# Self attention of a decoder block: queries and keys projected transposed, rotated pairs swapped and split parts stacked by SBUF-to-SBUF DMAs

## The chip, the cores and the metric

The kernel runs on one core of a Trainium2 chip. The time is the device time of one execution in microseconds (us): 1643.54 us before the change, the median of three runs (1643.11 to 1645.99). Engines are named as in the profile: PE is TensorE (matmuls; PEld its weight loads), DVE is VectorE, ACT is ScalarE, POOL is GpSimd, SP is SyncE, which here only issues DMAs.

## What is computed

A decoder block on x of 4 batches x 512 tokens x 512: self attention, cross attention over 1601 context rows, and a mixture of experts, each followed by residual and layer norm. The change touches self attention alone:

```python
q, k, v = (proj(Wq), proj(Wk), proj(Wv))          # 16 heads of 32
q = q * cos + _rotate_half(q) * sin               # _rotate_half: (x0, x1) -> (-x1, x0), pair by pair
k = k * cos + _rotate_half(k) * sin
att = softmax(q @ k.T / sqrt(32) + causal mask)
out = (att @ v).reshape(B, T, D) @ Wo.T
```

## The kernel before

Every matmul operand is split into a high part in fp32r and the rest in fp32r (`x_sp`, `wqkv`, `wo`, index 0 and 1), and a product is three matmuls (`PASSES`: hi*hi, hi*lo, lo*hi). For scores the three products are made in one matmul: for a head (32 features) the parts hi, hi, lo of q stand on 96 partitions above each other in `q_st`, and hi, lo, hi of k in `k_st`, so that one contraction over 96 rows sums all three.

The work goes in 16 groups, 4 heads of one batch each (`g = b * HG + hg`). For a group TensorE makes, in this order:

- 32 transposes (L496) of the split and rotated q and k (`qk_sp`, tokens on partitions) into `proj_ps`; ACT and DVE copy them to `q_st` (L253) and `k_st` (L362)
- `scores` (L446, the mask added by L448): 16 score tiles, n = qt * 4 + h, of 128 queries by 128 to 512 keys, in two PSUM buffers of `score_ps`; for each DVE takes the row maximum (L371, `maxed`), and the tile n waits for the maximum of n - 2
- the negated maxima are transposed (L520, `max_turned`) and copied as rows 96 to 127 of `q_st` (L260 on ACT, L391 on DVE), so that the second product comes out with the maximum subtracted
- `scores_t` (L462, mask L464): the scores again, keys on partitions; ACT takes the exponential (L268, `exped`) into `p_t`; behind it `values` (L471) and `weight_sums` (L478)

The projection of the next group (48 matmuls of 384 columns, L415: q, k and v of 4 heads for a token tile, tokens on partitions) is laid between these steps by hand, 5 matmuls behind each pair of scores, 7 and 6 around the first `scores_t`. When it is done ACT copies v (L232), DVE rotates (`rotate`, L305 to L312; the swap of pairs is a reversed access pattern on PSUM) and the parts are split by ACT, DVE and POOL (L201). Once a batch the output projection `project_out` (48 matmuls of 512 columns, L428) stands behind the scores of the next batch's first group.

SP loads x of a batch as one DMA, the weights in chunks through three places in `p_t`, and `rows` (4 MB, x by rows, for the residual), which is issued at 17.5 us. DVE waits for `rows_in` before its first group; PE starts when all weights are split (`w_lo`, 5 loads).

## Time and profile before

| | |
|---|---|
| median of 3 runs | 1643.54 us |
| the profiled execution: its span, first to last instruction | 1642.0 us |
| PE busy | 1421.5 us (87% of the span) |
| DVE, ACT, POOL busy | 993.8, 659.1, 271.0 us |
| mean granted TensorE clock | 0.937 of full speed |
| self attention: first matmul, last `weight_sums` | 26.4 us, 563 us |

A row of the timeline gives start, length, engine, line and operation, the tiles, the shape, the count of merged instructions, and in brackets how long the engine had been idle and what ended it. Matmuls overlap in their pipeline, so the time from one start to the next, not the length, is what one costs. PEclk is the granted clock of TensorE, 1.00 the upper of its two levels (2.4 GHz), 0.50 the lower (1.2 GHz). Self attention is a third of the span; what follows it (cross attention from 584 us, experts) begins when it has ended and is not changed.

### The profile page before, as it was taken

Reading aid. Unit: us, or ns where it says so; the run is one execution under the profiler, and the core shown is the slowest. Engines: PE = TensorE matmul, PEld = TensorE weight load, DVE = VectorE, ACT = ScalarE, POOL = GpSimd, SP = SyncE. Lnnn points to the kernel's source line nnn. Section 1 sums busy time; section 2 is a strip of 40 time slices with the busy share of each in tenths; the row PEclk is TensorE's granted clock in tenths of the full one; section 3 lists DMA queues with packets and bytes.
Section 4 is the critical chain, followed back from the end, with each engine's and each line's share of the span. In section 5 each row is a group of like instructions: output and inputs, shape, how many; then the busy total and the mean of one; then the engine's idle time right before and its main releaser. Section 6 shows DMA issues by size and latency. Waiting matters only on the chain. (4 is left out here: it accounts for less than half of the span.)

```text
span 1642.0 us, 25753 instructions
## 1 busy us (share of the span) xinstructions
PE 1421.5 (87%) x9093; PEld 1174.7 (72%) x9093; DVE 993.8 (61%) x1677; ACT 659.1 (40%) x1042; POOL 271.0 (17%) x233
## 2 busy tenths in 40 slices
PE   2898998998999758999898985499999999998890
PEld 2665676666766447788787874389999999997770
DVE  4665565565665483444434427777777777775677
ACT  3344233244334223333323314266566655664222
POOL 1002001001000020200102000122222222221762
PEclk9999999999999779999999998589999999999995
DMA  6000000000000032220312004177877878784654
GB/s 268 1 1 26 1 2 27 2 1 1 1 1 1 1 138 83 74 87 16 104 40 77 23 1 142 46 265 276 287 277 275 299 271 292 275 273 178 196 165 142
DMA packets 61589, 190.29 MB, mean 116 GB/s; under 512 B 7112, under 2 KB 7116, under 8 KB 60624
## 3 DMA queue, kind: packets, MB, share of 16 engines
q1 hardware_dynamic: 48880, 147.93, 24.6%
q0 software_dynamic: 12640, 41.43, 8.4%
q8 instruction: 45, 0.74, 0.2%
q14 instruction: 24, 0.20, 0.0%
HBM read 156.30 MB, written 33.03 MB: 115 GB/s over the span
## 5 line engine op out<-in xcount | busy, mean ns | idle before, releaser
L415 PE MATMUL proj_ps<-wqkv,x_sp 128*128 128x384 f32 x768 | 174.5, 362 | 26.4 <-DVE wo L297 26.4
L1510 DVE TENSOR_TENSOR e_w_sp<-e_w_raw,e_w_sp 128x1024 fp32r<-128x1024 f32 x141 | 168.7, 1221 | 18.1 <-ACT e_w_sp L1468 11.3
L952 PE MATMUL c_score_ps<-ct,x_t 128*128 128x402 f32 x768 | 155.4, 364 | 0.0
L952 PEld LDWEIGHTS c_score_ps<-ct,x_t 128*128 128x128 f32 x768 | 149.8, 201 | 6.9 <-issue 6.1
L1454 POOL DMA_INDIRECT e_x_g<-x_rows,e_index x94 | 101.2, 1076 | 323.7 <-DVE e_index L1521 309.1
L415 PEld LDWEIGHTS proj_ps<-wqkv,x_sp 128*128 128x128 f32 x768 | 135.2, 200 | 26.4 <-issue 26.4
L1468 ACT ACTIVATE e_w_sp<-e_w_raw 128x1024 fp32r<-128x1024 f32 x141 | 145.9, 1058 | 16.8 <-DMA e_w_raw<-w_experts 16.6
L992 PE MATMUL c_out_ps<-cr,weigh_t 128*128 128x512 f32 (+1 forms) x624 | 152.5, 399 | 0.0
L1569 PEld LDWEIGHTS e_gate_ps<-e_x_t,e_w_sp 128*128 128x128 f32 x1128 | 140.6, 191 | 5.9 <-DVE e_x_t L1531 1.8
L1569 PE MATMUL e_gate_ps<-e_x_t,e_w_sp 128*128 128x256 f32 x1128 | 142.1, 283 | 1.4 <-DVE e_x_t L1531 1.4
L1569 PE MATMUL e_up_ps<-e_x_t,e_w_sp 128*128 128x256 f32 x1128 | 143.3, 283 | 0.0
L371 DVE TENSOR_REDUCE row_max<-score_ps 128x1 f32<-128x128 f32 (+3 forms) x256 | 114.3, 483 | 47.8 <-PE score_ps L448 46.2
L1595 PE MATMUL e_down_ps<-e_w_sp,e_h_sp 128*128 128x512 f32 x564 | 139.0, 396 | 0.0
L1569 PEld LDWEIGHTS e_up_ps<-e_x_t,e_w_sp 128*128 128x128 f32 x1128 | 135.1, 188 | 0.0
L992 PEld LDWEIGHTS c_out_ps<-cr,weigh_t 128*128 128x128 f32 (+1 forms) x624 | 115.2, 188 | 25.7
L268 ACT ACTIVATE p_t<-score_ps 128x512 f32<-128x512 f32 (+3 forms) x256 | 102.2, 437 | 61.4 <-PE score_ps L464 59.6
L1595 PEld LDWEIGHTS e_down_ps<-e_w_sp,e_h_sp 128*128 128x128 f32 x564 | 102.6, 188 | 21.4
L877 DVE TENSOR_TENSOR weigh_t<-c_turn_ps,weigh_t 128x512 fp32r<-128x512 f32 x64 | 34.7, 584 | 134.1 <-ACT weigh_t L780 134.1
L780 ACT ACTIVATE weigh_t<-c_turn_ps 128x512 fp32r<-128x512 f32 x64 | 29.4, 513 | 196.5 <-PE c_turn_ps L973 196.5
L446 PE MATMUL score_ps<-k_st,q_st 96*128 96x256 f32 (+2 forms) x256 | 87.6, 399 | 16.8 <-POOL x_sp L195 8.6
L462 PE MATMUL score_ps<-q_st,k_st 128*128 128x256 f32 (+2 forms) x256 | 92.5, 413 | 8.5 <-ACT p_t L268 7.7
L462 PEld LDWEIGHTS score_ps<-q_st,k_st 128*128 128x128 f32 x256 | 50.2, 196 | 67.0 <-ACT p_t L268 62.4
(211 smaller groups left out, 2242.6 us busy)
## 6 DMA issues: line engine op xcount, KB each, us to landing
e_w_raw<-w_experts SPq DMA_DIRECT2D x141, 512.0 KB, 5.6
y_rows<-e_y SPq DMA_DIRECT2D x47, 512.0 KB, 2.9
raw<-ctxT SPq DMA_DIRECT2D x16, 800.5 KB, 4.3
raw<-ctx_rows SPq DMA_DIRECT2D x16, 768.0 KB, 4.8
x_raw<-xT SPq DMA_DIRECT2D x4, 1024.0 KB, 4.8
rows<-x_rows SPq DMA_DIRECT2D x1, 4096.0 KB, 14.2
x_rows<-rows SPq DMA_DIRECT2D x4, 1024.0 KB, 6.2
out<-rows SPq DMA_DIRECT2D x4, 1024.0 KB, 5.3
```

The source lines that it names most:

```text
L268: nc.scalar.activation(p_t[:, h, p_at[kc]:p_at[kc] + w], score_ps[:, n % 2, kc * P:T], ACT.Exp, scale=float(HD) ** -0.5).then_inc(exped, 1)
L371: nc.vector.tensor_reduce(row_max[:, qt, h:h + 1], score_ps[:, n % 2, 0:(qt + 1) * P], AX, ALU.max).then_inc(maxed, 1)
L415: mm = nc.tensor.matmul(proj_ps[:, tt, 0:GW], x_sp[:, xs, c, tt * P:(tt + 1) * P], wqkv[:, ws, c, hg * GW:(hg + 1) * GW], start=(c == 0 an ...
L446: nc.tensor.matmul(score_ps[:, n % 2, 0:wide], q_st[0:3 * HD, h, qt * P:w], k_st[0:3 * HD, h, 0:wide], start=True, stop=False)
L462: nc.tensor.matmul(score_ps[:, n % 2, q0:T], k_st[:, h, kc * P:(kc + 1) * P], q_st[:, h, q0:T], start=True, stop=False)
L952: mm = nc.tensor.matmul(score_ps[:, f, 0:MQ], x1_t[:, xs, c, qt * P:(qt + 1) * P], ct[:, cs, c, f * MQ:(f + 1) * MQ], start=False, stop=(c ...
L992: mm = nc.tensor.matmul(out_ps[:, qt % 2, :], weigh_t[0:k, ws, c, :], cr[0:k, cs, c, :], start=(c == 0 and m == 0), stop=(c == MC - 1 and ...
L1454: nc.gpsimd.indirect_dma_start(x_g[:, par, half, :], None, x2_rows, bass.IndirectOffsetOnAxis(ap=index[:, par, half:half + 1], axis=0)).th ...
L1468: nc.scalar.activation(w_sp[:, par, part, 0, :], w_raw[:, par, part, :], ACT.Copy).then_inc(w_hi[part], 1)
L1510: nc.vector.tensor_tensor(w_sp[:, par, part, 1, :], w_raw[:, par, part, :], w_sp[:, par, part, 0, :].bitcast(F32), ALU.subtract).then_inc( ...
L1569: mm = nc.tensor.matmul(ps[:, par, i, :], w_sp[:, par, part, ws, at:at + P], x_t[:, par, xs, c, :], start=(c == 0 and n == 0), stop=(c == ...
L1595: mm = nc.tensor.matmul(down_ps[:, half, :], h_sp[:, par, hs, i, half * P:(half + 1) * P], w_sp[:, par, DOWN, ws, i * D:(i + 1) * D], star ...
```

## The change

Queries and keys of 4 heads are projected with features on partitions and the 512 tokens along the row: weights are the stationary operand, 12 matmuls of 512 columns for q and 12 for k (L464 of the new kernel), into `qk_ps`. The values of a whole batch are projected apart, 48 matmuls of 512 columns (`project_v`; `values_ahead` behind the scores of the last group of the batch before; at the start in one pass with q and k). TensorE's transposes and the copies out of them are gone.

What was a reversed access pattern is now data movement over partitions: ACT copies the projection to `qk_raw`, SP issues two DMAs for each of q and k that swap even and odd partitions into `qk_swapped` (`swap`, 64 partitions x 2 KB each), POOL multiplies `qk_raw` by cos, DVE multiplies `qk_swapped` by sin and adds, ACT takes the high part, POOL the low part (into the place of `qk_swapped`). Then `put_together` fills `q_st` and `k_st`: for each head three DMAs for q and three for k, 24 DMAs of 32 partitions x 2 KB (64 KB) a group. As `q_st` and `k_st` exist once, SP waits before them for the last `scores_t` of the group before (`scored_t`, g * SC). Scores of heads 0 and 1 wait for the first 12 DMAs (`stacked[0]`), those of heads 2 and 3 for the second 12 (`stacked[1]`), and the next group's swap for all 24.

The output projection and the values use `job_ps`, two PSUM banks of their own. x comes in four DMAs a batch (into the free half of `v`), `woT` through `v` as well; `woT` and `rows` are issued behind `put_together(0)`. The loops over batches are written out.

```diff
+        def stack_places(h):
+
+            part = slice(h * HD, (h + 1) * HD)
+            for s, splits in ((Q, (hi, hi, lo)), (K, (hi, lo, hi))):
+                for n, src in enumerate(splits):
+                    yield stack[s][n * HD:(n + 1) * HD, h, :].bitcast(F32), src[part, s, :].bitcast(F32)
+
+        STACKED = 2 * 2 * 3 * 16
...
-                sp.dma_start(rows[:, :, :], x).then_inc(rows_in, 16)
-                with sp.Fori(1, B) as b:
-                    sp.wait_ge(x_lo, b)
-                    sp.dma_start(x_raw[:, :, :], xT[b]).then_inc(x_in, 16)
...
+                def swap(g, s):
+                    sp.wait_ge(copied, g * 2 + s + 1)
+                    if g >= 1:
+                        for pair in range(GH // 2):
+                            sp.wait_ge(stacked[pair], g * STACKED)
+                    for odd in range(2):
+                        sp.dma_start(swapped[odd:P:2, s, :], raw[1 - odd:P:2, s, :]).then_inc(swap_in[s], 16)
+
+                def put_together(g):
+                    sp.wait_ge(hi_done, g * 2 + 2)
+                    sp.wait_ge(lo_done, g * 2 + 2)
+                    if g >= 1:
+                        sp.wait_ge(scored_t, g * SC)
+                    for h in range(GH):
+                        for dst, src in stack_places(h):
+                            sp.dma_start(dst, src).then_inc(stacked[h // 2], 16)
+
...
+                swap(0, Q)
+                swap(0, K)
+                put_together(0)
+                sp.wait_ge(x_lo, DC)
+                sp.dma_start(v[:, 1, :, :].rearrange("p t d -> p (t d)"), woT).then_inc(wo_in[0], 16)
+                sp.dma_start(rows[:, :, :], x).then_inc(rows_in[0], 16)
+                for g in range(NG - 1):
+                    b, hg = g // HG, g % HG
+                    swap(g + 1, Q)
+                    swap(g + 1, K)
+                    if hg == 1 and b + 1 < B:
...
+                    put_together(g + 1)
...
+                def times_cos(g, s):
+                    pool.wait_ge(swap_in[s], (g + 1) * 32)
+                    if g == 0:
+                        pool.wait_ge(tables_in, 32)
+                    nc.gpsimd.tensor_tensor(raw[:, s, :], raw[:, s, :], cos_t[:, :], ALU.mult).then_inc(by_cos, 1)
+
+                def lo_qk(g, s):
+                    pool.wait_ge(hi_done, g * 2 + s + 1)
+                    nc.gpsimd.tensor_tensor(lo[:, s, :], raw[:, s, :], hi[:, s, :].bitcast(F32), ALU.subtract
+                                            ).then_inc(lo_done, 1)
...
+                def copy_raw(g, s):
+                    act.wait_ge(projected, g * 2 + s + 1)
+                    if g >= 1:
+                        act.wait_ge(lo_done, (g - 1) * 2 + s + 1)
+                    nc.scalar.activation(raw[:, s, :], qk_ps[:, s, :], ACT.Copy).then_inc(copied, 1)
+
+                def hi_qk(g, s):
+                    act.wait_ge(rotated, g * 4 + 2 * s + 2)
+                    if g >= 1:
+                        for pair in range(GH // 2):
+                            act.wait_ge(stacked[pair], g * STACKED)
+                    nc.scalar.activation(hi[:, s, :], raw[:, s, :], ACT.Copy).then_inc(hi_done, 1)
...
-                            if n == 1 and not last:
-                                keep_v(g + 1, (hg + 1) % 2)
+                            if n == GH + 1 and not last:
+                                hi_qk(g + 1, Q)
                             if n == 2 * GH + 1 and not last:
-                                hi_q(g + 1)
...
-                        nc.vector.tensor_tensor(qk_cos[:, s, :, :], proj_ps[:, :, part], cos_t[:, :, :],
-                                                ALU.mult).then_inc(roped, 1)
-                        swapped = proj_ps[:, :, part].rearrange("p t (n two) -> p t n two", two=2)[:, :, :, ::-1]
-                        nc.vector.tensor_tensor(qk_sin[:, s, :, :].rearrange("p t (n two) -> p t n two", two=2),
-                                                swapped, sin_t[:, :, :].rearrange("p t (n two) -> p t n two", two=2),
-                                                ALU.mult).then_inc(roped, 1)
...
+                def rotate(g, s):
+                    dve.wait_ge(swap_in[s], (g + 1) * 32)
+                    if g == 0:
+                        dve.wait_ge(tables_in, 32)
+                    nc.vector.tensor_tensor(swapped[:, s, :], swapped[:, s, :], sin_t[:, :], ALU.mult
+                                            ).then_inc(rotated, 1)
+                    dve.wait_ge(rotated, g * 4 + 2 * s + 1)
+                    dve.wait_ge(by_cos, g * 2 + s + 1)
+                    nc.vector.tensor_tensor(raw[:, s, :], raw[:, s, :], swapped[:, s, :], ALU.add
+                                            ).then_inc(rotated, 1)
...
-                    dve.wait_ge(scored_t, g * GH * TT)
-                    for h in range(GH):
-                        dve.wait_ge(turned, g * 2 * GH + 2 * h + 2)
-                        nc.vector.tensor_copy(k_st[0:3 * HD, h, :], proj_ps[0:3 * HD, (2 * h + 1) % 4, :]
-                                              ).then_inc(k_stacked, 1)
...
+                for s in (Q, K):
+                    rotate(0, s)
+                dve.wait_ge(*rows_in)
+                for g in range(NG):
+                    b, hg = g // HG, g % HG
+                    last = g == NG - 1
+                    if g >= 1:
+                        for part in range(3):
+                            invert_sums(g - 1, part)
+                        finish_out(g - 1)
...
-                            if n % 2 == 1 and n < 2 * GH and not first:
-                                if n // 2 < 3:
-                                    invert_sums(g - 1, n // 2)
-                                elif n // 2 == 3:
-                                    finish_out(g - 1)
...
-                products = [(tt, c, n) for tt in range(TT) for c in range(DC) for n in range(3)]
-
-                def project(g, hg, start, stop):
-
-                    for tt, c, n in products[start:stop]:
-                        xs, ws = PASSES[n]
-                        mm = nc.tensor.matmul(proj_ps[:, tt, 0:GW], x_sp[:, xs, c, tt * P:(tt + 1) * P],
-                                              wqkv[:, ws, c, hg * GW:(hg + 1) * GW],
+                products = [(c, n) for c in range(DC) for n in range(3)]
+                jobs = [0]
+
+                def project(g, s, start, stop):
+
+                    at = s * D + g % HG * P
+                    for c, n in products[start:stop]:
+                        ws, xs = PASSES[n]
+                        mm = nc.tensor.matmul(qk_ps[:, s, :], wqkv[:, ws, c, at:at + P], x_sp[:, xs, c, :],
                                               start=(c == 0 and n == 0), stop=(c == DC - 1 and n == 2))
-                        if c == DC - 1 and n == 2:
-                            mm.then_inc(projected, 1)
+                    if stop == len(products):
+                        mm.then_inc(projected, 1)
...
+                def project_v(b, tt, into, chunks=range(DC)):
+
...
+                                                  wqkv[:, ws, c, 2 * D:3 * D], start=(c == 0 and n == 0),
...
+                def values_ahead(b):
+
+                    if b == 1:
+                        pe.wait_ge(v_copied, TT)
+                    else:
+                        pe.wait_ge(res_added, (b - 1) * TT)
+                    pe.wait_ge(x_lo, split_x(b, DC - 1))
+                    for tt in range(TT):
+                        if tt >= 2:
+                            pe.wait_ge(v_copied, b * TT + tt - 1)
+                        project_v(b, tt, job_ps)
...
+                    if qt == 0:
+                        pe.wait_ge(stacked[h // 2], (g + 1) * STACKED)
+                    if n >= 2:
+                        pe.wait_ge(maxed, g * SC + n - 1)
+                    elif g >= 1:
+                        pe.wait_ge(exped, g * SC)
+                    else:
+                        pe.wait_ge(v_copied, TT)
...
-                    for n in range(2 * GH):
-                        h, s = n // 2, n % 2
-                        if n == 1:
-                            pe.wait_ge(k_lo, g + 1)
-                        if n >= 4:
...
-                        for tt in range(TT):
-                            mm = nc.tensor.transpose(proj_ps[0:3 * HD, n % 4, tt * P:(tt + 1) * P].bitcast(F32R),
-                                                     qk_sp[:, s, tt, h, :, :].rearrange("p n d -> p (n d)"),
-                                                     ident_r[:, :])
-                        mm.then_inc(turned, 1)
...
+                for c in range(DC):
+                    pe.wait_ge(w_lo, c + 1)
+                    pe.wait_ge(x_lo, c + 1)
+                    for s in (Q, K):
+                        project(0, s, c * 3, c * 3 + 3)
+                    for tt in range(TT):
+                        project_v(0, tt, (job_ps, score_ps)[tt // 2], [c])
+                pe.wait_ge(const_ready, 3)
+                for g in range(NG):
+                    b, hg = g // HG, g % HG
+                    last = g == NG - 1
+                    if not last:
+                        pe.wait_ge(copied, g * 2 + 1)
+                        if hg == HG - 1:
+                            pe.wait_ge(x_lo, split_x(b + 1, DC - 1))
+                        project(g + 1, Q, 0, len(products))
+                        pe.wait_ge(copied, g * 2 + 2)
+                    for n in range(SC):
+                        scores(g, n // GH, n % GH)
+                        if not last and n < len(products):
+                            project(g + 1, K, n, n + 1)
+                    if hg == 0 and b >= 1:
+                        project_out(b - 1)
                     if hg == HG - 1 and not last:
-                        pe.wait_ge(x_lo, b + 2)
-                    STEP = 5
-                    for n in range(2 * TT):
-                        scores(g, n // 2, n % 2)
-                        if n == 1 and not last:
-                            pe.wait_ge(q_stacked, g * GH + GH)
-                            pe.wait_ge(k_stacked, g * GH + GH)
-                        if n >= 1 and not last:
-                            project(g + 1, (hg + 1) % HG, (n - 1) * STEP, n * STEP)
-                    if hg == 0 and not first:
-                        project_out(b - 1)
-                    at = (2 * TT - 1) * STEP
-
-                    pe.wait_ge(max_lo, g + 1)
-                    if hg == 0 and not first:
-                        pe.wait_ge(res_added, b * TT)
-                    pe.wait_ge(o_scaled, g)
+                        values_ahead(b + 1)
+
+                    pe.wait_ge(negated, g * 2 + 2)
+                    if g >= 1:
+                        pe.wait_ge(o_scaled, g)
                     for qt in range(TT):
                         mm = nc.tensor.transpose(den_ps[:, qt * P:(qt + 1) * P].bitcast(F32R),
                                                  neg_max[:, qt, :, :].rearrange("p h n -> p (h n)"), ident_r[:, :])
                     mm.then_inc(max_turned, 1)
-                    if not last:
-                        project(g + 1, (hg + 1) % HG, at, at + 7)
-                    pe.wait_ge(maxed, g * GH * TT + GH * TT)
-                    scores_t(g, 0, 0)
-                    if not last:
-                        project(g + 1, (hg + 1) % HG, at + 7, len(products))
-                    scores_t(g, 0, 1)
+                    pe.wait_ge(maxed, g * SC + SC)
+                    for half in range(2):
+                        scores_t(g, 0, half)
+                    if g == 0:
+                        pe.wait_ge(v_copied, TT)
                     for kc in range(1, TT):
                         scores_t(g, kc, 0)
-                        values(g, hg, kc - 1)
+                        values(g, kc - 1)
                         scores_t(g, kc, 1)
                         weight_sums(g, kc - 1)
-                    values(g, hg, TT - 1)
+                    values(g, TT - 1)
                     weight_sums(g, TT - 1).then_inc(summed, 1)
-
-                pe.wait_ge(const_ready, 3)
-                pe.wait_ge(w_lo, W_LOADS)
-                pe.wait_ge(x_lo, 1)
-                project(0, 0, 0, len(products))
-                groups(group, lambda: project_out(B - 1))(pe)
+                project_out(B - 1)
```

SyncE, from the third weight chunk to the `rows` load, before:

```order
L167 DMA p_t<-wqkvT 128x1536 x3
L169 DMA cos_t<-rope 128x512
L170 DMA sin_t<-rope 128x512
L167 DMA p_t<-wqkvT 128x1536
L167 DMA p_t<-woT 128x2048
L171 DMA rows<-x_rows 128x8192
```

and the same place now: after the last weight chunk the swaps of group 0 (four DMAs in one row), the stacking of its four heads (the six rows from L175 `x2` on are one head), and only then `woT` and `rows`:

```order
L181 DMA p_t<-wqkvT 128x1536
L166 DMA qk_swapped<-qk_raw 64x512 x4
L175 DMA q_st<-qk_hi 32x512 x2
L175 DMA q_st<-qk_swapped 32x512
L175 DMA k_st<-qk_hi 32x512
L175 DMA k_st<-qk_swapped 32x512
...
L189 DMA v<-woT 128x2048
L190 DMA rows<-x_rows 128x8192
L166 DMA qk_swapped<-qk_raw 64x512 x4
```

28 DMAs have come ahead of `woT` and `rows`, and 28 more follow for every further group.

TensorE, from the last 512-wide score tile of a group (L446 before, L518 now) to the first tiles of the second product (L462, L534), before:

```order
L446 MATMUL score_ps<-k_st,q_st 128x512
L448 MATMUL score_ps<-mask_qk,ident_b 128x128
L415 MATMUL proj_ps<-wqkv,x_sp 128x384 x5
L520 MATMUL den_ps<-ident_r,neg_max 128x128 x4
L415 MATMUL proj_ps<-wqkv,x_sp 128x384 x7
L462 MATMUL score_ps<-q_st,k_st 128x512
```

and now:

```order
L518 MATMUL score_ps<-k_st,q_st 128x512
L520 MATMUL score_ps<-mask_qk,ident_b 128x128
L587 MATMUL den_ps<-ident_r,neg_max 128x128 x4
L534 MATMUL score_ps<-q_st,k_st 128x512
L536 MATMUL score_ps<-mask_kq,ident_b 128x128
```

No projection stands between these steps any more: q's 12 matmuls stand ahead of the group's scores, k's one by one behind the first 12 score tiles.

## Rows read from the trace of the kernel before

**Rows 1.** The first line of the page
```profile
span 1642.0 us, 25753 instructions
```

**Rows 2.** Windows: two whole groups and a stretch of the last; columns in its first line
```profile
core 0: us, PE busy (x) PEld busy (x) DVE busy (x) ACT busy (x) POOL busy (x), PEclk, DMA share, GB/s
...
504.28:533.15 28.87, 27.27 (x216) 19.17 (x213) 18.46 (x36) 11.78 (x25) 2.56 (x2) 1.00 0.00 1
...
533.15:563.00 29.85, 25.33 (x168) 14.17 (x164) 13.39 (x29) 10.68 (x23) 1.27 (x1) 0.77 0.00 1
...
541.70:555.30 13.60, 11.34 (x36) 5.43 (x35) 5.77 (x11) 4.54 (x8) 1.21 (x1) 0.50 0.01 2
```

**Rows 3.** Timeline of TensorE, second group, last but one: start, length, what, count
```profile
73.24 2.67 PE L496 MATMUL proj_ps<-ident_r,qk_sp 128*96 128x128 f32 x32
...
503.11 0.23 PE L464 MATMUL score_ps<-mask_kq,ident_b 128*128 128x128 bf16 x1
...
504.28 2.68 PE L496 MATMUL proj_ps<-ident_r,qk_sp 128*96 128x128 f32 x32
...
519.41 1.45 PE L415 MATMUL proj_ps<-wqkv,x_sp 128*128 128x384 f32 x7
...
520.71 0.40 PE L462 MATMUL score_ps<-q_st,k_st 128*128 128x512 f32 x1
```

**Rows 4.** Timeline of TensorE, the last group
```profile
535.66 0.35 PE L446 MATMUL score_ps<-k_st,q_st 96*128 96x256 f32 x1
...
536.89 0.35 PE L446 MATMUL score_ps<-k_st,q_st 96*128 96x256 f32 x1 [0.56 <-DVE row_max L371]
...
547.22 0.75 PE L520 MATMUL den_ps<-ident_r,neg_max 128*128 128x128 f32 x4 [1.22 <-DVE neg_max L383]
...
562.41 0.40 PE L478 MATMUL den_ps<-p_t,ones 128*32 128x128 f32 x8
```

**Rows 5.** Timeline of the SP queue: issues that follow each other at once
```profile
2.95 0.44 SPq L169 DMA_DIRECT2D cos_t<-rope  x1
...
3.44 0.49 SPq L170 DMA_DIRECT2D sin_t<-rope  x1
...
582.92 1.29 SPq L697 DMA_DIRECT2D raw<-ctxT  x3
```

**Rows 6.** DMA issues by line: count, KB each, us from issue to landing
```profile
bias<-expert_bias SPq DMA_DIRECT2D x1, 8.0 KB, 1.8
...
rows<-x_rows SPq DMA_DIRECT2D x1, 4096.0 KB, 14.2
```

**Rows 7.** Timeline of TensorE at a batch boundary
```profile
269.11 0.58 PE L446 MATMUL score_ps<-k_st,q_st 96*128 96x256 f32 x1 [2.90 <-POOL x_sp L195]
```

**Rows 8.** Timeline of the start, several engines
```profile
5.69 1.91 ACT L226 ACTIVATE x_sp<-x_raw 128x2048 fp32r<-128x2048 f32 x1 [3.56 <-DMA x_raw<-xT]
...
7.76 1.48 ACT L282 ACTIVATE wqkv<-p_t 128x1536 fp32r<-128x1536 f32 x1 [0.17 <-DMA p_t<-wqkvT]
...
19.50 1.76 DVE L297 TENSOR_TENSOR wqkv<-p_t,wqkv 128x1536 fp32r<-128x1536 f32 x1 [2.35 <-ACT wqkv L282]
...
26.42 10.09 PE L415 MATMUL proj_ps<-wqkv,x_sp 128*128 128x384 f32 x48 [26.42 <-DVE wo L297]
...
47.65 0.47 DVE L371 TENSOR_REDUCE row_max<-score_ps 128x1 f32<-128x128 f32 x2
```

**Rows 9.** Groups by line and shape, self attention: busy us, mean ns; idle before
```profile
L232 ACT ACTIVATE v<-proj_ps 128x512 f32<-128x512 f32 x15 | 9.0, 597 | 5.1 <-PE proj_ps L415 5.1
...
L201 POOL TENSOR_TENSOR qk_sp<-qk_cos,qk_sp 128x512 fp32r<-128x512 f32 x15 | 19.2, 1282 | 273.7 <-ACT qk_sp L238 273.7
...
L305 DVE TENSOR_TENSOR qk_cos<-proj_ps,cos_t 128x512 f32<-128x512 f32 x30 | 20.6, 688 | 34.1 <-ACT v L232 17.9 <-PE proj_ps L415 16.2
```

**Rows 10.** Timeline of TensorE, output projection of the last batch
```profile
572.62 2.96 PE L428 MATMUL den_ps<-wo,o_sp 128*128 128x512 f32 x12
...
575.42 2.96 PE L428 MATMUL o_ps<-wo,o_sp 128*128 128x512 f32 x12
```

382 lines of the change are left out of this document (189 added, 193 removed).

## The prediction

> **What bounds the kernel now.** I read the windows over whole groups first, then TensorE's timeline inside one, then the SP queue and the landings. In a group in the middle of self attention TensorE is busy 27.27 of 28.87 us at the full granted clock [rows 2]: it is the bound, because projection matmuls of the next group fill its waits for DVE's maxima and ACT's exponentials. The last group has nothing to fill with: it takes 29.85 us though it makes 48 matmuls fewer, and for 13.60 us of it the granted clock is 0.50 [rows 2]. That group is my model for the new one. Self attention ends at 563 us of a span of 1642.0 us [rows 1, 2]; what follows starts when it has ended and keeps its length.
>
> **Removed from TensorE.** The 32 transposes of a group go: 2.5 us (504.28 to 506.8, one 2.68 us piece less its pipeline [rows 3]). A 384-column matmul costs (520.71 - 519.41) / 7 = 0.186 us [rows 3], a 512-column one (575.42 - 572.62) / 12 = 0.233 us [rows 10]. Before 48 x 0.186 = 8.9 us of projection a group; now 24 x 0.233 = 5.6 us a group and 48 x 0.233 = 11.2 us a batch for the values, together 8.4. As work this is 3.0 us a group less. ACT and DVE lose four copies each, which only TensorE's next step waited for.
>
> **Added: the stacking wait.** I call T the end of a group's `weight_sums`. The last `scores_t` of a group starts at 503.11 and is done 0.9 us before T = 504.28 [rows 3]; only then may SP begin the 24 stacking DMAs. It issues them in order, and an issue occupies SP: three in a row took 1.29 us, 0.43 each, two loads of 2 KB rows started 3.44 - 2.95 = 0.49 apart [rows 5]. Theirs have 128 partitions, these 32; I take 0.41. The low bound is the 0.23 us that 64 KB take at the rate of the 4096 KB load (14.2 us [rows 6]), the high one 0.49. From last issue to landing I take 2.0 us: 1.8 for 8 KB [rows 6] and 0.2 for the bytes. So the first 12 DMAs have landed at T - 0.9 + 11 x 0.41 + 2.0 = T + 5.6, all 24 at T + 10.5. TensorE has only q's projection in between, 12 x 0.233 = 2.8 us: it waits from T + 2.8 to T + 5.6, does two score tiles, and waits for the third until T + 10.5. Some 7 us a group have no cover. Everything else of the new chain does: q is copied and swapped while SP and DVE wait anyway, k's projection ends with the twelfth tile, and swap, cos (POOL 1.28), sin and sum (DVE 0.69 each), the splits (ACT 0.60, POOL 1.28) [rows 9] come to some 8 us against more than 12 us from there to the last `scores_t`. If that cover failed, ACT would stand at `hi_qk` with the exponentials queued behind it, and `scores_t` with them. The next swap is queued on SP behind all 24 DMAs, which delays nothing that is late.
>
> **Added: the lost filling.** From the third score tile to the end the last group takes 562.4 - 536.9 + 0.3 = 26 us [rows 4], half of it at clock 0.50. The new group has this stretch with ten of k's matmuls in it (2.3 us at the full clock, most inside waits for maxima), and DVE's inversion of the sums moved ahead of the tiles, where the stacking wait covers it (some 1 us less). I take 27 us. The clock: TensorE got 0.50 from 541.70 on after several short waits [rows 2], and at a batch boundary a wait of 2.90 us [rows 7] came before half-speed matmuls; every new group has two such waits, so half the stretch at 0.50 stays in my 27. Bounds: 24 (full clock nearly throughout) and 31 (half throughout).
> A new group is then 10.5 + 27 = 37.5 us against 28.87: +8.6.
>
> **Batches.** Three times 11.2 us of values come in as a block of their own behind the scores: +33.5. Their block covers the wait for the maxima, 1.2 us and the clock around it [rows 4]: -4.5. Before, the 14 groups from 73.24 to 533.15 [rows 2, 3] took 459.9 us, where 14 x 28.87 + 3 x 11.2 (output projection) are 437.8: 22 us went at batch boundaries, mostly in the wait for POOL's split of x [rows 7] and the half clock behind it. The new order splits x two groups ahead in four pieces: -21.
>
> **The start.** TensorE now begins when a first chunk is split: 1 MB lands by 5.69, then ACT's split of 1.48 and DVE's of 1.76 [rows 8], so at 9 instead of 26.4, with 72 x 0.233 + 1.1 us of slow start (48 x 0.186 took 10.09 before [rows 8]), q and k ready at 24. Copies 1.2, swap 2.8, the rotation and splits as above give 32.6; 24 issues end at 42.5. Only then `woT` and `rows` are issued, and DVE does not take a maximum before `rows` has landed, 14.2 us later [rows 6]: 57 against 47.65 before [rows 8]. With 0.6 for two maxima and 27 the second group begins at 84.7, before at 73.24: +11.5.
>
> **Sum.** Start +11.5; 14 groups x 8.6 = +120; batches +33.5 - 4.5 - 21 = +8; the last group 10.5 + 25.5 = 36 against 29.85: +6. Together +145.5, so the profiled execution's 1642.0 becomes 1788, and the median of the runs, 1.5 above it, 1789.
>
> The Trainium skill bears on the dearest term twice. "DMA: Bandwidth & Descriptors", section "Issuing engines are not separate DMA queues", holds the sequencer's time for starting a DMA to be usually small beside the transfer. By these rows it is not: 0.43 us of issue against 0.23 us of bytes. By that rule the stacking would run at the transfers' pace, the second rival below. "SBUF — State Buffer", section "The DMA setup-cost knee", says a loop of 64 KiB transfers moves about 30% of what one of 4 MiB does; from its 395 GB/s an estimate of 0.55 us a DMA, 24 landed at T + 13.8, and the sum would be 1789 + 3.3 x 15 = 1838. No run here shows 64 KB DMAs yet.
>
> **Rivals.**
> 1. The waits vanish (issues of about 0.1 us). Nothing in the rows speaks for it: the shortest mean issue is 0.43. Then a group is 2.8 + 0.3 + 26.5 = 29.6, +0.7 x 14 = 10, with start +8, batches +8 and the last group -2: 1642 + 24, so 1667. 0.07.
> 2. The transfers set the pace, not the issues: 23 x 0.23 = 5.3, all landed at T + 6.4, a group of 33.4. 15 x 4.1 = 61 less, 4 less at the start: 1724. For it: these DMAs have a quarter of the rows of those in the trace. Against: issues in the trace differ little between loads of 256 KB and 800 KB. 0.15.
> 3. Slower than forecast: rows of 2 KB among 32 partitions go below the rate of the big load, or the half clock holds through the group (31): 10.5 + 31 or 14.5 + 27 are +4 a group, 15 x 4 = 60: 1849. For it: the granted clock of the last group. 0.15.
> 4. The other side, faster: TensorE stays busy as now and takes only its work. Its place is the score phase: it decides if stacks land before T + 2.8, 24 DMAs in 2 us, and the removed 3.0 us a group are not lost again to maxima and exponentials. Then 16 x 3.0 = 48 and the 21 of the boundaries are saved, the start gains nothing: 1643.5 - 69 = 1574. Against it the last group before, which lost to these waits all that 48 matmuls had cost. 0.03.
> 5. The change does not do what it says: not likely here; the DMAs are in the program in the order that the text shows.
>
> **How the numbers follow.** My forecast has 0.60. Its own range is 1750 to 1835 (issue 0.35 to 0.47, stretch 26 to 29). The range for 8 in 10 goes from rival 2 to rival 3 with a margin for 24 and 31 together with them: 1705 to 1865. A measurement of this kernel tells 0.2% (3 us) from no change. Faster only by rival 4 and a corner of rival 1: 0.04; within 0.2%: 0.01; slower: 0.95.
>
> **What would show it.** In the changed trace: SP's stacking issues about 0.41 us apart, beginning within 0.2 us of a group's last `scores_t`; TensorE idle before the first score tile about 2.8 us and before the third about 4 us, released by DMA, in each of 15 groups; group periods near 37.5 us; the clock 0.50 in a large part of them, mean below 0.937; the first maximum of DVE near 57 us, released by `rows`; self attention ending near 709 us; everything behind it as long as before. I am wrong if the period is below 33 us (issues faster, or the clock holds), or if TensorE's longest waits name ACT or DVE instead of a DMA (the rotation chain is late after all).

## The result and the profile after

| | before | after |
|---|---|---|
| median of four runs | 1644.76 us (1643.11 to 1646.12) | 1875.01 us (1871.06 to 1876.39) |
| ratio, 95% interval | | 1.1397 [1.138, 1.1413] |
| span of the profiled execution, mean granted clock | 1642.0 us, 0.937 | 1874.6 us, 0.859 |
| end of self attention | 563 us | 796 us |

The forecast was 1789 us with 1705 to 1865 for 8 in 10. The sign was right, and the time lies 10 us above the range. All of the loss is in self attention (796 - 563 = 233 us, as much as the spans differ).

The first lines of the page after, against [rows 1]:

```profile
span 1874.6 us, 24131 instructions
PE 1477.0 (79%) x8389; PEld 1149.6 (61%) x8389; DVE 935.6 (50%) x1548; ACT 649.6 (35%) x1038; POOL 348.2 (19%) x294
```

TensorE's timeline at the joint of two groups in the middle, where [rows 3] are of before (L464 is q's projection, L518 a score tile):

```profile
370.42 0.41 PE L545 MATMUL o_ps<-p_t,v 128*32 128x128 f32 x8
370.64 0.40 PE L552 MATMUL den_ps<-p_t,ones 128*32 128x128 f32 x8
370.98 3.01 PE L464 MATMUL qk_ps<-x_sp,wqkv 128*128 128x512 f32 x12
379.19 0.55 PE L518 MATMUL score_ps<-k_st,q_st 96*128 96x256 f32 x1 [5.20 <-issue]
380.21 0.41 PE L518 MATMUL score_ps<-k_st,q_st 96*128 96x256 f32 x1
...
386.77 0.58 PE L518 MATMUL score_ps<-k_st,q_st 96*128 96x256 f32 x1 [5.47 <-DMA k_st<-qk_hi]
```

With T = 370.98, the first score tile starts at T + 8.2 and the third at T + 15.8. The forecast had T + 5.6 and T + 10.5. SP's queue over the same joint, 12 issues of the 24 shown:

```profile
370.12 1.19 SPq L175 DMA_DIRECT2D q_st<-qk_hi  x2
371.36 0.59 SPq L175 DMA_DIRECT2D q_st<-qk_swapped  x1
371.99 0.59 SPq L175 DMA_DIRECT2D k_st<-qk_hi  x1
372.62 0.59 SPq L175 DMA_DIRECT2D k_st<-qk_swapped  x1
373.26 0.59 SPq L175 DMA_DIRECT2D k_st<-qk_hi  x1
373.89 1.22 SPq L175 DMA_DIRECT2D q_st<-qk_hi  x2
375.15 0.60 SPq L175 DMA_DIRECT2D q_st<-qk_swapped  x1
...
384.66 0.59 SPq L175 DMA_DIRECT2D k_st<-qk_hi  x1
386.80 1.15 SPq L166 DMA_DIRECT2D qk_swapped<-qk_raw  x2
```

An issue occupies SP for 0.59 us, and the next starts 0.63 us after it began; this distance is called the pitch below. The 24 of them from 370.12 to 385.25 take 15.1 us, where 24 x 0.41 = 9.8 were forecast. The first starts 0.3 us after the last `scores_t` tile (369.81). The landings, from the page, answer to [rows 6]:

```profile
qk_swapped<-qk_raw SPq DMA_DIRECT2D x64, 128.0 KB, 2.1
q_st<-qk_hi SPq DMA_DIRECT2D x128, 64.0 KB, 2.0
k_st<-qk_hi SPq DMA_DIRECT2D x128, 64.0 KB, 2.0
```

TensorE's longest waits from 100 to 800 us (total, times, longest):

```profile
PE score_ps L518 <- DMA k_st<-qk_hi: 92.3, 16, 8.1
PE score_ps L518 <- issue: 75.3, 14, 6.5
PE den_ps L587 <- DVE neg_max L434: 13.2, 9, 2.3
```

"issue" at L518 is the wait before the first score tile: TensorE waits for `stacked[0]`, and the profile names no event for it. The two together are 168 us. One group, from its first score tile to the next group's, cut at the third, answers to [rows 2]:

```profile
379.19:386.77 7.58, 2.10 (x7) 1.20 (x7) 0.58 (x2) 0.00 (x0) 0.00 (x0) 0.50 0.39 97
386.77:422.10 35.33, 33.29 (x190) 21.54 (x191) 13.31 (x23) 11.59 (x25) 5.12 (x4) 0.92 0.05 18
```

At the start the first maximum waits for `rows`, which SP could issue only behind the stacks ([rows 8] for before):

```profile
50.94 0.46 SPq L190 DMA_DIRECT2D rows<-x_rows  x1
65.45 0.49 DVE L427 TENSOR_REDUCE row_max<-score_ps 128x1 f32<-128x128 f32 x2 [32.77 <-DMA rows<-x_rows]
```

### The profile page after: what moved, and what is told of

Its sections match the earlier page's. It is cut to its first block and busy times, and to the rows that moved or that the text cites. A ratio compares the mean times of both kernels' runs of the same rounds, so it can differ in the third digit from the quotient of the medians.

```text
span 1874.6 us, 24131 instructions
## 1 busy us (share of the span) xinstructions
PE 1477.0 (79%) x8389; PEld 1149.6 (61%) x8389; DVE 935.6 (50%) x1548; ACT 649.6 (35%) x1038; POOL 348.2 (19%) x294
## 5 line engine op out<-in xcount | busy, mean ns | idle before, releaser
L518 PE MATMUL score_ps<-k_st,q_st 96*128 96x256 f32 (+2 forms) x256 | 114.4, 450 | 205.3 <-DMA k_st<-qk_hi 92.3
L427 DVE TENSOR_REDUCE row_max<-score_ps 128x1 f32<-128x128 f32 (+3 forms) x256 | 122.4, 490 | 281.4 <-PE score_ps L520 243.3
L518 PEld LDWEIGHTS score_ps<-k_st,q_st 96*128 96x128 f32 x256 | 66.3, 259 | 230.9 <-issue 115.0
L464 PE MATMUL qk_ps<-x_sp,wqkv 128*128 128x512 f32 x384 | 170.5, 523 | 9.3 <-DVE wqkv L365 9.3
L282 ACT ACTIVATE qk_raw<-qk_ps 128x512 f32<-128x512 f32 x32 | 19.1, 597 | 348.3 <-PE qk_ps L464 348.2
L534 PE MATMUL score_ps<-q_st,k_st 128*128 128x256 f32 (+2 forms) x256 | 116.1, 504 | 20.8 <-ACT q_st L339 13.2
L534 PEld LDWEIGHTS score_ps<-q_st,k_st 128*128 128x128 f32 x256 | 59.3, 232 | 97.0 <-issue 48.5
L464 PEld LDWEIGHTS qk_ps<-x_sp,wqkv 128*128 128x128 f32 x384 | 91.2, 241 | 19.4 <-DVE wqkv L365 9.2
```

The lines of the kernel that those rows point to most:

```text
L427: nc.vector.tensor_reduce(row_max[:, qt, h:h + 1], score_ps[:, n % 2, 0:(qt + 1) * P], AX, ALU.max).then_inc(maxed, 1)
L464: mm = nc.tensor.matmul(qk_ps[:, s, :], wqkv[:, ws, c, at:at + P], x_sp[:, xs, c, :], start=(c == 0 and n == 0), stop=(c == DC - 1 and n = ...
L518: nc.tensor.matmul(score_ps[:, n % 2, 0:wide], q_st[0:3 * HD, h, qt * P:w], k_st[0:3 * HD, h, 0:wide], start=True, stop=False)
L534: nc.tensor.matmul(score_ps[:, n % 2, q0:T], k_st[:, h, kc * P:(kc + 1) * P], q_st[:, h, q0:T], start=True, stop=False)
```

## The experiments

All ratios are to the kernel before, run on the same chip, with a 95% interval. Times are medians of four to six runs, but single runs where this is said. A "plain" group has no block of 48 matmuls (values or output projection).

**Fewer, larger DMAs.** High and low parts lie in one tensor, q's and k's stacks in another, so that one DMA serves both.

```diff
-            for s, splits in ((Q, (hi, hi, lo)), (K, (hi, lo, hi))):
-                for n, src in enumerate(splits):
-                    yield stack[s][n * HD:(n + 1) * HD, h, :].bitcast(F32), src[part, s, :].bitcast(F32)
+            for n, src in enumerate((slice(0, 3, 2), slice(0, 4, 3), slice(1, 3, 1))):
+                yield stack[n * HD:(n + 1) * HD, :, h, :].bitcast(F32), parts[part, src, :]
```

> The four parts of q and k lie in one tensor and q_st and k_st in another, so that one DMA of 32 partitions x 2 x 2 KB takes the place of two: 12 stacking DMAs of 128 KB a group instead of 24 of 64 KB, same bytes. Theory A (an SBUF-to-SBUF issue costs SP 0.63 us whatever it moves): the stacks have landed 12 x 0.63 = 7.6 us earlier in each of 16 groups, 1875 - 16 x 7.6 = about 1753, issues still 0.63 apart. Theory B (the pace is that of bytes or packets, the queue pushes back): issues 1.26 apart and 1875 as now. The swaps, 128 KB each and 0.62 apart in the changed kernel's trace, speak for A.

1761.76 us, ratio 1.0708 [1.069, 1.0726]. Half the DMAs with twice the bytes: the pitch stays.

```profile
411.75 8.06 SPq L175 DMA_DIRECT2D qk_st<-qk_parts  x12
```

Twelve in 8.06 us are 0.67 each (7.7 to 7.8 in most groups, 0.65). On one queue, and up to 128 KB, the number of DMAs sets the cost and not the bytes.

**A second queue.** Heads 2 and 3 are issued by ACT, unmerged.

```diff
-                    for h in range(GH):
+                    for h in range(GH // 2):
...
+                    for h in range(GH // 2, GH):
+                        for dst, src in stack_places(h):
+                            act.dma_start(dst, src).then_inc(stacked[h // 2], 16)
```

> The 24 stacking DMAs are split: heads 0 and 1 issued by SP, heads 2 and 3 by ACT behind its last exponential of the group, nothing else changed. Theory A (each issuing engine needs 0.63 us of its own a DMA): both halves run side by side, the third score tile comes about 7.6 - 1.7 = 6 us earlier in 15 groups, about 1785. Theory B (the DMA rings or a shared generator set the pace): no gain, 1875, with issues on both engines about 1.26 apart.

1779.73 us, 1.0814 [1.0796, 1.0832]. Two queues issue side by side; over one group's twelve issues the pitch was 0.65 us on ACT and 0.68 on SP. The wait moved in part: `PE score_ps L530 <- ACT qk_raw L282` is 48.5 us in 9 times, since ACT copies q only after its issues.

**No stacks after the first group** (later groups compute with the first group's).

```diff
-                    put_together(g + 1)
```

> The stacking DMAs are left out for all groups but the first; later groups take their scores from the first group's stacks (the output is not the reference's). Swaps, rotation and splits stay. This measures the wait for the stacks apart from the lost filling. Theory 1 (the whole loss is the stacking wait): a group falls to below the 28.87 us of the kernel before and the time to some 1600. Theory 2 (my terms): a group is 2.8 + 0.3 + 27 = 30, up to 2.5 less if the clock now holds; 14 groups x 13.5 us off 1875 and about 12 in the last: about 1675, so still slower than before by 30.

1660.17 us, 1.0098 [1.0082, 1.0115]. So the stacking costs 215 of the 230 us; what is left of the change is 15. Rival 1 of the prediction, the waits gone, had 1667 for this case, with 29.6 us for a group; the plain groups took 28.3 in the mean.

**Rows first.** `rows` is issued ahead of the first swap.

```diff
+                sp.dma_start(rows[:, :, :], x).then_inc(rows_in[0], 16)
                 swap(0, Q)
...
-                sp.dma_start(rows[:, :, :], x).then_inc(rows_in[0], 16)
```

> The load of rows (4 MB) is issued behind the last weight chunk, ahead of the swaps of the first group, instead of behind its stacking. Theory (DVE's wait for rows in front of the first maximum is part of the miss): the first maxima come at 44.8 and the third at 52.5, when the second stacks land, instead of 65.4 and 66.6: 13 us less, 1862. Rival: rows only takes the place of another wait, because the swaps stand behind it in the rings: no change or up to 5 us worse.

1860.66 us, 1.1322 [1.1297, 1.1346]: 14 us, and they are the start's (first maximum at 45.82 instead of 65.45).

**Other shapes of DMA, by group** (groups 1 and 2 issue 16 small loads from DRAM besides, groups 3 to 10 leave out or misplace part of the stacks). In the order of the lines: 96 partitions with a third of the columns, 32 partitions without change of place, 32 partitions with rows of 512 B, 16 partitions with rows of 2 KB.

```diff
+                            if g in (3, 4):
+                                x = sp.dma_start(stack[s][0:3 * HD, h, cols].bitcast(F32), hi[0:3 * HD, s, cols].bitcast(F32))
+                            elif g in (5, 6):
+                                x = sp.dma_start(stack[s][rows_n, h, :].bitcast(F32), hi[rows_n, s, :].bitcast(F32))
+                            elif g in (7, 8):
+                                x = sp.dma_start(stack[s][rows_n, h, 0:128].bitcast(F32), hi[part, s, 0:128].bitcast(F32))
+                            elif g in (9, 10):
+                                x = sp.dma_start(stack[s][n * HD:n * HD + 16, h, :].bitcast(F32), hi[h * HD:h * HD + 16, s, :].bitcast(F32))
```

> What an issue costs, measured by itself: the changed kernel with stacking DMAs of other shapes in some groups (the output is not the reference's): DRAM to 32 partitions x 512 B, SBUF to SBUF with 96 partitions, with 32 partitions that do not change place, with rows of 512 B, with 16 partitions. Theory A (a DMA that reads and writes SBUF costs its queue 0.63 whatever its shape): 0.63 for all but the DRAM ones, those 0.35 to 0.45. Theory B (the partitions' crossing or the number of rows costs): less where they stay in place or are 16. Theory C (few partitions cost, not the source): the DRAM ones take 0.63 as well.

The run took 1887.86 us (one run); only its issues count here. In order: 32 x 512 B rows from DRAM in two groups, then from SBUF the stacks as they are, and 96 partitions (L188):

```profile
99.94 1.81 SPq L180 DMA_DIRECT2D scratch<-xT  x4
144.93 7.29 SPq L180 DMA_DIRECT2D scratch<-xT  x16
153.49 0.59 SPq L196 DMA_DIRECT2D q_st<-qk_swapped  x1
195.01 1.84 SPq L188 DMA_DIRECT2D q_st<-qk_hi  x3
```

And the durations of single issues, minimum, median and maximum in ns, by shape (L190 same partitions, L192 512 B rows, L194 16 partitions):

```profile
L188 SPq DMA_DIRECT2D q_st<-qk_hi x24: 549/595/605, 195.0 to 258.0; - x24
L190 SPq DMA_DIRECT2D q_st<-qk_hi x24: 556/591/829, 298.1 to 354.3; - x24
L192 SPq DMA_DIRECT2D q_st<-qk_hi x24: 555/591/1076, 386.2 to 449.4; - x24
L194 SPq DMA_DIRECT2D q_st<-qk_hi x24: 556/589/598, 489.2 to 545.2; - x24
```

From DRAM 7.29 / 16 = 0.46 us an issue, from SBUF 0.63 (0.59 and 0.04 between two), with 16, 32 or 96 partitions, rows of 512 B or 2 KB, 16 to 64 KB. At equal shape, 32 rows of 512 B, only the source differs. The forecast's rows were all loads from DRAM.

**Merged and on two queues** (SP heads 0 and 2, ACT 1 and 3).

```diff
-                    for h in range(GH):
+                    for h in (0, 2):
...
+                    for h in (1, 3):
+                        for dst, src in stack_places(h):
+                            act.dma_start(dst, src).then_inc(stacked[h // 2], 16)
```

> The merged stacking DMAs (12 of 128 KB a group) and two issuing queues together: SP issues heads 0 and 2, ACT heads 1 and 3, six each at 0.63 us. If the issue time of each queue is all there is, the first pair has landed at T - 0.9 + 2 x 0.63 + 2.0 = T + 2.4, all at T + 4.3, against T + 8.0 in the run with merged DMAs on SP alone: 3.7 us less in 15 groups and the clock better held, about 1762 - 56 = 1706, down to 1690. If the transfers set the pace once the issues do not, little under 1762.

1761.94 us, 1.0727 [1.0704, 1.075]: nothing over the merged parts on one queue, and the expectation fell. Both queues now take 1.0 us an issue:

```profile
408.17 6.04 SPq L175 DMA_DIRECT2D qk_st<-qk_parts  x6
```

```profile
408.20 5.80 ACTq L298 DMA_DIRECT2D qk_st<-qk_parts  x6
```

The windows of that stretch say why (the last two columns are the busy share of the DMA engines and GB/s):

```profile
410.00:412.00 2.00, 2.00 (x9) 1.33 (x8) 1.57 (x3) 0.00 (x0) 0.00 (x0) 1.00 0.90 189
412.00:414.00 2.00, 0.04 (x1) 0.00 (x0) 0.00 (x0) 0.00 (x0) 0.00 (x0) 1.00 0.96 237
414.00:416.00 2.00, 1.20 (x6) 0.71 (x6) 0.58 (x2) 1.12 (x2) 0.71 (x1) 0.97 0.99 216
```

**The same with half the bytes** tests it (columns 256 to 511 stay the first group's).

```diff
-                        for dst, src in stack_places(h):
+                        for dst, src in stack_places(h, T // 2 if g else T):
```

> The run with merged parts and both queues again, but from the second group on each stacking DMA moves only the first 256 of its 512 columns (1 KB rows, 64 KB a DMA instead of 128 KB); the other columns stay those of the first group. Theory A, the bytes set the pace there: in that run six issues took 6.0 us on each queue, a DMA landed 4.4 us after its issue, and the DMA engines were busy 0.94 of 410 to 415 us. With half the bytes the pitch falls back to 0.63 on each queue and the landing to about 2.1 us: the last stack lands 5 x 0.63 + 2.1 = 5.3 us after the first issue instead of 5 x 1.0 + 4.4 = 9.4, 4 us less in 14 or 15 groups, 1762 - 58 = about 1704. Theory B, two queues that issue such DMAs hinder each other whatever the bytes: pitch stays near 1.0, landing near 4.4, the time within 1755 to 1765.

1684.12 us (one run). Six issues take 4.2 us, a landing 2.2 us instead of 4.4, and the DMA engines' share in the two windows of 2 us with most traffic is 0.81 and 0.64. The bytes did set the pace. The gain of 78 us is larger than the 58 expected; the mean granted clock rose too, from 0.884 to 0.901, and what part is the clock's is not shown.

**The lost filling, alone**: the kernel before with its 48 projection matmuls in one block ahead of the scores.

```diff
+                    if not last:
+                        pe.wait_ge(q_stacked, g * GH + GH)
+                        pe.wait_ge(k_stacked, g * GH + GH)
+                        project(g + 1, (hg + 1) % HG, 0, len(products))
                     for n in range(2 * TT):
                         scores(g, n // 2, n % 2)
...
-                        if n >= 1 and not last:
-                            project(g + 1, (hg + 1) % HG, (n - 1) * STEP, n * STEP)
```

> The kernel before with one part of the change alone: the 48 projection matmuls of the next group in one block ahead of the scores instead of between them; transposes, copies, no stacking DMAs. Theory (filling hides the projection): each of 15 groups grows from 28.87 to the last group's 29.85 plus the block of 8.9 and 1 us of waiting for the copies, about +11, to some 1643 + 15 x 10.5 = 1800, less where the block keeps the clock up. Rival (TensorE's work is the bound and the order does not matter): within 20 us of 1643.

1799.95 us, 1.0957 [1.0935, 1.098]. The order of matmuls among waits was worth 155 us to the kernel before. Some 10 of them belong to a wait that the block brings with it, for the copies into `k_st` ahead of it (9.6 us in 11 times from 50 to 700 us).

**All mends**: merged, two queues, rows first, values and output projection three matmuls at a time behind score tiles 2 to 13, k's projection behind tiles 4 to 15.

```diff
+                        if 2 <= n < 14:
+                            if hg == 0 and b >= 1:
+                                project_out(b - 1, (n - 2) * 3, (n - 1) * 3)
+                            if hg == HG - 1 and not last:
+                                values_ahead(b + 1, (n - 2) * 3, (n - 1) * 3)
```

> Merged DMAs, two queues and the early load of rows, and filling put back: k's 12 projection matmuls stand behind score tiles 4 to 15 instead of 0 to 11, the values' and the output projection's 48 are laid three by three behind tiles 2 to 13 with the last 12 behind all, ACT splits x of the next batch among the exponentials. From the run before: rows 14 us, six blocks of 48 that now hide DVE's maxima some 3 us each, k behind the long reductions 1 us a group: 1700 - 14 - 18 - 15 = about 1655. If the lost filling was not a cost, no less than 1690. Under 1644 it would beat the kernel before.

1743.23 us, 1.0596 [1.0579, 1.0614]: a miss by 88 us. 62 us of it stood in the number it started from: 1700 was the forecast for the merged DMAs on two queues, which took 1762. The rest is the filling and `rows`: they brought 19 us where 47 were expected. TensorE still waits twice, since two queues with 128 KB a DMA run at the pace of the bytes:

```profile
436.65 0.35 PE L543 MATMUL score_ps<-qk_st 96*128 96x256 f32 x1 [2.44 <-issue]
440.03 0.58 PE L543 MATMUL score_ps<-qk_st 96*128 96x256 f32 x1 [2.70 <-DMA qk_st<-qk_parts]
```

**Rows and filling without stacks** (from the kernel with the first group's stacks).

> Leaves out the stacking DMAs after the first group (later groups compute with the stacks of the first), with rows issued early and the filling put back (k's projection among tiles 4 to 13, values and output projection three by three behind tiles 2 to 13). It says what the stacks cost in the kernel with all the mends, and whether the mended order without them would beat the kernel before. Theory A: as in the step from the two queues to all mends the filling and the rows give some 19 us, so 1660 - 19 = 1641, ratio about 0.998. Rival: without the stack wait the filling is worth more, since now nothing else spends the time in which maxima are waited for: the groups with 48 more matmuls go from 37 to about 31, 6 x 6 = 36, and 14 us from rows: about 1610, ratio 0.98.

1635.16 us, 0.9941 [0.9924, 0.9958]; between the two theories, nearer the first. Plain groups take 27.1 to 28.5 us (28.9 before). The groups with a block of 48 still take 35 to 39 us, and 36 to 39 in the kernel with only the stacks left out, so laying the blocks among the tiles brought little. With these mends only the stacks stand between the change and the old time.

**Another order: heads by pairs.** Scores, exponentials and values run through heads 0, 1 first, then 2, 3. The first pair's stacks are free half a phase earlier, the second pair's are needed half a phase later.

```diff
-                    if g >= 1:
-                        sp.wait_ge(scored_t, g * SC)
                     for h in range(GH):
+                        if g >= 1 and h % 2 == 0:
+                            sp.wait_ge(scored_t, (g - 1) * SC + (h // 2 + 1) * 2 * TT)
...
-                        scores(g, n // GH, n % GH)
+                        scores(g, n // 2 % TT, n // (2 * TT) * 2 + n % 2)
```

> The changed kernel with its 24 stacking DMAs of 64 KB from SP, but scores, exponentials, values and weight sums run through heads 0, 1 first (all four tiles of each) and then heads 2, 3, and the high parts of the next group are made after the exponentials 2 and 6 instead of 6 and 10. So the 12 DMAs of heads 0, 1 can be issued when the eighth transposed score tile is done, some 6 us before the last, and the 12 of heads 2, 3 are first needed at the ninth score tile. Theory A (the queue's 0.63 us an issue is what costs, and it can be hidden where it lies beside other work): heads 0, 1 are issued by 1.6 us after the last transposed score tile, heads 2, 3 7.6 us later and landed at 11.2 us, which is 10.3 us after the end of the weight sums, where TensorE comes to the ninth tile after about 8: a group falls from 43.5 to about 33, the time to about 1725. Rival (the wait is only moved: the third tile's wait becomes one of the same length at the ninth, since the 24 issues still take 15.1 us): about 41 a group, 1840.

1739.66 us, 1.0577 [1.0561, 1.0593]; plain groups 33.4 to 36.4. The 24 issues of 0.63 are all still there, and 135 us are gone: much of their cost lay in the place of the wait.

**Pairs and all mends**, on one queue.

> The same order by pairs of heads with the merged parts (12 DMAs of 128 KB, all from SP), the rows issued early and the filling put back (k's projection at tiles 2 to 13). Theory A: heads 0, 1 are issued in 3.9 us before the group's last transposed score tile, heads 2, 3 in the 3.9 us after it and land 6.3 us after it, before TensorE comes to the ninth score tile. No stacking wait is left, and the time comes near that of the same mends without any stacks, 1635: 1632 to 1645, ratio 0.992 to 1.0. Rival: the stacks' transfers and the swaps behind them on the SP queue delay the rotation (swap of q issued 7 us after the end of a group instead of at once), so that a wait for POOL or ACT takes the place of some 2 us a group: about 1665, ratio 1.012.

1704.19 us, 1.0348 [1.0327, 1.0369]: both theories fell. No stacking wait is left (the first score tile waits 0.2 us at most after q's projection, the ninth not at all), and yet a plain group takes 31.5 to 33.6 us. A pair of rows of weight sums, both at the full granted clock, gives part of it. By pairs:

```profile
436.52 1.03 PE L567 MATMUL den_ps<-p_t,ones 128*32 128x512 f32 x4
```

and all four heads, in the kernel without stacks:

```profile
421.42 1.06 PE L565 MATMUL den_ps<-p_t,ones 128*32 128x512 f32 x8
```

Four matmuls take as long as eight. Each gives 32 partitions of output; the reading is that those of four heads run side by side and those of two leave half unused.

**Values and sums for four heads again**, behind the second pair's tiles.

```diff
                     for m in range(2 * TT):
                         scores_t(g, m % TT, m // TT)
                         if m > TT:
                             values(g, m - TT - 1)
                             weight_sums(g, m - TT - 1)
```

> As the run by pairs of heads with all mends, but values and weight sums are again computed for all four heads together, a key chunk at a time, behind the transposed score tiles of heads 2, 3. Theory A (matmuls whose output has 32 columns of the array run beside those of the other heads: in the run with all mends and no stacks eight of 512 columns took 1.06 us for four heads, in the run by pairs four took 1.07 us for two heads, so by pairs these cost twice as much): values and weight sums take 1.06 + 0.85 + 0.60 + 0.39 = 2.9 us each, 5.8 us a group instead of 11.6; some of it goes into waits for the exponentials of heads 0, 1, which nothing fills now. A plain group falls from 31.5 to about 28, the time from 1704 to about 1704 - 15 x 3.5 = 1650, ratio about 1.003. Rival (the loss is the half clock after waits inside the transposed scores, not the columns): with nothing among the first eight tiles the waits grow, the period stays 31 or more, 1695 to 1710.

1676.72 us, 1.0201 [1.0187, 1.0215]: a gain of 27 us, half of what was expected. Where the granted clock is full the eight take 1.03 to 1.04 us again, but only three groups have that; in most they take 1.8 to 1.9. The first pair's tiles now stand bare, and the clock falls (404 to 416 us; columns as above):

```profile
404.00:416.00 12.00, 10.99 (x36) 5.57 (x40) 3.74 (x6) 8.67 (x20) 7.70 (x7) 0.50 0.00 0
```

**Filling them**: q's projection two groups ahead behind the first pair's tiles, k's as a block behind score tile 1.

```diff
+                        if m < TT and g + 2 < NG and hg != HG - 2:
+                            project(g + 2, Q, m * 3, m * 3 + 3)
```

> As the run before (pairs of heads, values and weight sums for four heads together), but q's projection is made two groups ahead, three matmuls behind each of the first four pairs of transposed score tiles (not where the next batch's x isn't split yet), and k's projection as one block behind the first two score tiles, where DVE inverts the sums. There is as much work as before. Theory A (the rest of the loss is half clock: in the run before, 404 to 416 us of a group's transposed scores ran at a granted clock of 0.50, with little between waits for exponentials): the twelve matmuls fill those waits, the stretch keeps the full clock, a group loses some 2.5 us: 1676 - 12 x 2.5 = 1646, ratio 1.001. Rival (the clock does not come back, or falls in the score tiles that now stand without k's matmuls): the period stays near 31 or grows by the wait for DVE's inversion, 1670 to 1690.

1650.7 us, 1.0047 [1.0033, 1.0062]: 26 us gained by place alone, nearly theory A's time, though not where it put the gain. Of four groups of a batch three are shorter (29.6, 33.7, 36.5 against 30.8, 38.3, 42.9); the one without q two groups ahead (`hg == HG - 2`) is longer, 33.8 against 31.2, with 12 us at half clock. Most of the gain is in the two groups with a block of 48, of which one (305 to 342 us) now has the full clock throughout. The plain one gains 1.3 us and still has the stretch from 220 to 226 us at 0.50. How much is due to q's matmuls and how much to k's block was not tried apart. This version has every stack of the changed kernel and is within 0.5% of the kernel before, on its slower side; none with all its stacks beats it.

## Why the prediction was wrong

Right, by its own steps: the bound of before and what fills TensorE; the first issue 0.3 us behind the start of the last `scores_t` tile; the landing (2.0 us, taken 2.0); the stretch from the third score tile of a group to its end (27.4 us, 343.60 to 370.98, and 27.5 in the mean of the eight plain groups; taken 27); the rotation hidden; the start of TensorE (9.25 against 9); the waits before the first and the third tile, with a DMA as releaser of the third; everything behind self attention as long as before (it ends 1079 us before the end of the span in both).

The step that failed is the issue pitch: "I take 0.41", between 0.23 and 0.49. It measured 0.63. The terms, in the profiled execution, from the end of one group's `weight_sums` to that of the next (T), rest on these rows:

```profile
94.74 3.01 PE L464 MATMUL qk_ps<-x_sp,wqkv 128*128 128x512 f32 x12
343.60 0.58 PE L518 MATMUL score_ps<-k_st,q_st 96*128 96x256 f32 x1 [5.49 <-DMA k_st<-qk_hi]
753.24 0.40 PE L552 MATMUL den_ps<-p_t,ones 128*32 128x128 f32 x8
795.42 0.40 PE L552 MATMUL den_ps<-p_t,ones 128*32 128x128 f32 x8
```

| term | forecast | measured | difference |
|---|---|---|---|
| start, to the second group | 84.7 | 94.7 | +10 |
| the 14 groups behind the first (94.7 to 753.6) | 587.9 | 658.9 | +71 |
| last group | 36 | 42 | +6 |
| sum of the change | +145.5 | +232.6 | +87 |

A group's second twelve wait on 23 pitches, 23 x (0.63 - 0.41) = 5.1 us, and 71 / 14 is 5.1. The last group has the same 5.1, and the start has 24 issues before `rows` can go, 5.3 of its 10. So one number makes about 82 of the 87 us. The rest is of the start: the stacking began at 35.12 instead of 32.6, and the stretch from the third tile took 28.9 us instead of 27. Mechanism and count were right; the size was not, and its upper bound was no bound: every row it came from was a load from DRAM, and none was a DMA from SBUF to SBUF.

That the 14 groups come out so exactly is in part luck. The eight plain ones took 43.5 us in the mean, from first score tile to first score tile, where 37.5 + 5.1 are 42.6; over 14 groups that is 12 us too little. The six groups with a block of 48 together took 50 us more than plain ones, where the sum had 64 (33.6 + 33.5 - 4.5 + 1). The two errors cancel.

With 0.63 the prediction's own sum gives 1642 + 145.5 + 15 x 5.1 + 5.3 = 1869 for the span.

The rivals. The waits did not vanish, and the removed work did not come out as time. The transfers as pace (1724) did not come: doubling the bytes left the pitch at 0.65. It did come true once issues were spread over two queues with 128 KB each, at 216 to 237 GB/s and 0.96 to 0.99 of the engines' share; I had missed that in expecting 1706 of that run. Slower than forecast (1849) was the nearest number, but neither of its mechanisms is what happened: no low rate, and 27.4 us in the stretch, not 31. The estimate by the Trainium skill, "SBUF — State Buffer", "The DMA setup-cost knee" (0.55 us a DMA, 1838), was nearer than mine: the trace has 0.63 for 64 KB. It is a figure for one size; here 128 KB on one queue took 0.65 us, and 16 partitions x 2 KB took 0.63. The Trainium skill, "DMA: Bandwidth & Descriptors", "Issuing engines are not separate DMA queues", holds that a second issuing engine saves only the time of the issue, usually small beside the DMA. By these runs it was not small (0.63 us against an estimated 0.23 of bytes): it was the limit, and a second issuing engine took 95 us off. That all DMAs share the same 16 engines, as the section also says, agrees with the run of merged DMAs on two queues, where the bytes were the limit.

What the change cost, by these runs: 1875 - 1660 = 215 us by the stacking (168 of them waits before the two score tiles; the mean granted clock is 0.859 with stacks and 0.906 without, and what part of the rest is the clock's is not shown), 1660 - 1635 = 25 by `rows` and the filling (`rows` alone gave 14 in the kernel with stacks), and 1645 - 1635 = 10 gained by the rest. That 15 us remain without stacks is shown; how the 10 divide between the transposes that went and the boundaries of batches is not.

## What to carry to other kernels

A price for a DMA's issue holds for its kind of source and target: take it from a row of the same kind, or leave the upper bound wide. Where a buffer exists once, DMAs that fill it cost by the place of the wait as well as by their time: the same 24 issues cost 135 us less when half of them went under work that was there anyway, and half the issues at the old place cost 113 us less. Before moving work between engines, look at what it had filled: where the matmuls of the kernel before stood, among waits, was worth some 155 us.

## What the hardware showed

- An issue of a DMA from SBUF to SBUF occupied SP for 0.59 us with 0.04 between two, for 16 to 96 partitions, 512 B to 2 KB rows, 16 to 64 KB; 0.65 an issue with 128 KB. One of 32 rows of 512 B from DRAM took 0.46.
- SP and ACT issued side by side at 0.65 to 0.68 us each with 64 KB a DMA (32 rows of 2 KB), and at 1.0 with 128 KB, where the DMA engines were 0.90 to 0.99 busy. A DMA of 128 KB landed 2.4 us after its issue from one queue and 4.4 from two.
- Matmuls of 128 rows into 32 output partitions: eight for four heads took 1.06 us, four for two heads 1.03 (512 columns, granted clock 1.00).
- The granted clock stayed at 0.50 for 12 us in which TensorE was busy 10.99 of 12.00, with short waits between tiles; in the last run it was 1.00 from 330 to 336 us, where TensorE was busy 5.07 of 6.00.
